# Attention scores of two heads in the two row halves of TensorE's array, with keys that hold no zero blocks

## What is computed

```python
# x: (2, 1024, 256); ctx: (2, 154, 192); 16 heads of 64 features
h = layernorm(x)
q = (h @ Wq).reshape(B, N, 16, 64).transpose(0, 2, 1, 3)
k = (ctx @ Wk).reshape(B, 154, 16, 64).transpose(0, 2, 1, 3)
v = (ctx @ Wv).reshape(B, 154, 16, 64).transpose(0, 2, 1, 3)
sim = einsum('bhid,bhjd->bhij', q, k) * 64 ** -0.5
attn = softmax(sim, axis=-1)
o = einsum('bhij,bhjd->bhid', attn, v)
x = x + tanh(g_xattn) * (o @ Wo + bo)
x = x + tanh(g_ffn) * moe(layernorm(x))   # top 2 of 8 experts, silu gate
```

## Time and profile before

| | |
|---|---|
| timed runs, median of 3 | 596.3 us (595.17 to 599.48) |
| profiled execution, its span (its own time is not told apart) | 602.2 us |
| PE busy (weight loads: 476.4) | 522.3 us, 87% |
| DVE busy | 340.4 us, 57% |
| ACT busy | 282.2 us, 47% |
| POOL busy | 231.9 us, 39% |

### The profile page before, as it was taken

The page is one execution under the profiler, slowest core; times in us unless marked ns, Lnnn a source line. Parts: engine busy times, 40 slices in busy tenths (PEclk is TensorE's granted clock), DMA queues, the critical chain, the costliest instruction groups (busy, mean ns, idle before and its releaser), DMA issues.

```text
span 602.2 us, 12363 instructions
## 1 busy us (share of the span) xinstructions
PE 522.3 (87%) x3712; PEld 476.4 (79%) x3713; DVE 340.4 (57%) x783; ACT 282.2 (47%) x866; POOL 231.9 (39%) x319
## 2 busy tenths in 40 slices
PE   8999999999999999998998420699988998999991
PEld 6789999998989889898998410588877877888881
DVE  5856666677586585765756764255444544533330
ACT  3446556555465555564553112355543544533330
POOL 5160000337008780077704625043433433443333
PEclk9999999999999999999999755799999999999995
DMA  8500000001000100001010995636446436333322
GB/s 246 181 2 1 0 2 2 20 1 35 3 0 26 44 20 15 0 10 63 2 36 1 224 229 178 206 84 151 109 90 156 117 76 157 53 51 53 55 36 26
DMA packets 32372, 41.54 MB, mean 69 GB/s; under 512 B 3088, under 2 KB 28432, under 8 KB 32336
## 3 DMA queue, kind: packets, MB, share of 16 engines
q1 hardware_dynamic: 25184, 31.75, 17.9%
q0 software_dynamic: 7152, 9.33, 9.9%
HBM read 24.12 MB, written 16.95 MB: 68 GB/s over the span
## 4 chain that ended last, share of the span: by engine, by line
PE 34%; issue 26%; DVE 11%; ACT 8%; DMA 6%; POOL 6%; POOLq 3%; DVEq 2%; SPq 2%; another core or an unknown queue 1%; ACTq 0%
PE bank L603 7%; PE bank L581 6%; ACT probs L773 5%; PE bank L527 4%; POOL tok L1225 4%; PE bank L543 4%; PE bank L1279 3%; PE bank L557 3%; DMA expert_queue<-zrow 3%; DVE nmax L892 2%; POOLq L1233 2%; DMA out_dram<-yq,to_row 2%; PE bank L706 2%; PE bank L501 2%; DVEq L902 1%
## 5 line engine op out<-in xcount | busy, mean ns | idle before, releaser
L773 ACT ACTIVATE probs<-bank,nmax 128x154 f32<-128x154 f32 x256 | 97.6, 388 | 123.6 <-DVE nmax L892 119.3
L581 PE MATMUL bank<-vdiag,pT 128*128 128x128 f32 (+2 forms) x640 | 80.0, 272 | 7.1 <-DVE oT_lo L916 6.9
L581 PEld LDWEIGHTS bank<-vdiag,pT 128*128 128x128 f32 (+1 forms) x640 | 77.5, 191 | 10.5 <-DVE oT_lo L916 10.3
L1234 POOL DMA_INDIRECT out_dram<-yq,to_row x39 | 61.8, 1585 | 33.7 <-issue 24.1
L1279 PE MATMUL bank<-gu_hi,xqT_hi 128*128 x156 | 68.7, 441 | 1.1 <-DVE xqT_lo L1396 1.1
L892 DVE TENSOR_REDUCE nmax<-bank 128x2 f32<-128x308 f32 x128 | 60.1, 471 | 7.7 <-PE bank L543 6.8
L1279 PE MATMUL bank<-gu_hi,xqT_lo 128*128 x156 | 61.9, 397 | 0.0
L1279 PE MATMUL bank<-gu_lo,xqT_hi 128*128 x156 | 61.7, 396 | 0.0
L1408 DVE TENSOR_TENSOR hidT_lo<-bank,hidT_hi 128x512 fp32r<-128x512 f32 x39 | 26.9, 690 | 53.1 <-ACT hidT_hi L1355 53.1
L1403 DVE TENSOR_TENSOR hid<-hid,bank 128x512 f32<-128x512 f32 x39 | 26.8, 688 | 52.6 <-PE bank L1279 52.6
L557 PE MATMUL bank<-ident,probs 128*128 128x128 f32 (+1 forms) x320 | 46.2, 273 | 5.6 <-ACT xfT L786 2.9
(11 more groups left out here) (183 smaller groups left out, 1432.4 us busy)
## 6 DMA issues: line engine op xcount, KB each, us to landing
gu_raw<-in_gate_up_wT_dram SPq DMA_DIRECT2D x8, 1024.0 KB, 5.0
expert_queue<-zrow SPq DMA_DIRECT2D x8, 642.5 KB
xq<-expert_queue SPq DMA_DIRECT2D x39, 128.5 KB, 2.5
dn_raw<-in_down_wT_dram SPq DMA_DIRECT2D x8, 512.0 KB, 6.0
x<-in_x_dram SPq DMA_DIRECT2D x4, 512.0 KB, 13.0
out_dram<-out SPq DMA_DIRECT2D x8, 256.0 KB, 2.2
wq_raw<-in_L_xattn_Wq_dram SPq DMA_DIRECT2D x1, 1024.0 KB, 11.5
wo_raw<-in_L_xattn_Wo_dram SPq DMA_DIRECT2D x1, 1024.0 KB, 10.6
```

Of the source, the lines that this page charges most:

```text
L581: last = nc.tensor.matmul(at[:, col0 + j0 * DH:col0 + j0 * DH + n], pT[u % 2][0:rows, b, :], v, start=(b == 0), stop=(b == NBLK - 1), skip ...
L773: last = nc.scalar.activation(probs[u % 4][:, j * NKB:(j + 1) * NKB], S_BANK[hf][:, m * NKB:(m + 1) * NKB], ACT.Exp, bias=nmax[:, u % 4, j ...
L1234: nc.gpsimd.indirect_dma_start(out[:, :], bass.IndirectOffsetOnAxis(to_row[:, 0:1], 0), yq[p % 2][:, :], None, compute_op=ALU.add).then_in ...
```

## The change

The keys lose their zero blocks: `k_hi` and `k_lo` have 154 columns for a pair and batch, the first head in rows 0 to 63 and the second in rows 64 to 127, as PE makes them. The scores of a head are a matmul of 64 array rows and 154 columns: heads of the first half of a pair (`side` 0) go through rows 0 to 63 into `S_BANK[0]`, those of the second half (`side` 1) through rows 64 to 127 into `S_BANK[1]`, in turn. The position in the array follows from the partitions of the operands. A unit has 12 such matmuls in place of 6, and each has its own weight load. Bank 0 now holds the first heads of both pairs, bank 1 the second heads; the maxima write `nmax` with a stride of two and the exponentials find head `2 * m + side` in place `m` of a bank.

All 12 score matmuls of a unit are issued in one piece, ahead of the transpositions, and both semaphores `s["exp"][0]` and `s["exp"][1]` are waited for ahead of the first. ACT and DVE keep their order. The keys are split by one instruction of 128 partitions on ACT and one on DVE, and the memsets of zero blocks and their semaphore are gone. (In the changed file lines stand up to twelve earlier.)

```diff
-            k_hi = asb("k_hi", [P, H // 2, B, 2 * NKB], F32R)
-            k_lo = asb("k_lo", [P, H // 2, B, 2 * NKB], F32R)
+            k_hi = asb("k_hi", [P, H // 2, B, NKB], F32R)
+            k_lo = asb("k_lo", [P, H // 2, B, NKB], F32R)
...
-                for half, keys in zero_keys:
-                    nc.gpsimd.memset(k_lo[half, :, :, keys].bitcast(F32), 0.0).then_inc(s["k_zero"], 1)
-                    nc.gpsimd.drain()
...
                 def scores(i, u):
 
                     par, w = (u // 8) % 2, u % 8
-                    for hf in range(2):
-                        at_least(pe, s["exp"][hf], UPI * i + u)
-                        if w < UPT and hf == 0:
-                            pe.wait_ge(s["proj_sb"][w + 1], GPI * i + u // 8 + 1)
-                        pair = (u % UPT) * 2 + hf
-                        tok = ((u // UPT) % 2) * P
+                    for side in range(2):
+                        at_least(pe, s["exp"][side], UPI * i + u)
+                    if w < UPT:
+                        pe.wait_ge(s["proj_sb"][w + 1], GPI * i + u // 8 + 1)
+                    tok = ((u // UPT) % 2) * P
+                    for m in range(2):
+                        pair = (u % UPT) * 2 + m
                         n = 0
                         for q, k in ((q_hi, k_hi), (q_hi, k_lo), (q_lo, k_hi)):
-                            last = nc.tensor.matmul(S_BANK[hf][:, 0:2 * NKB], q[par][:, pair, tok:tok + P], k[:, pair, par, :],
-                                                    start=(n == 0), stop=(n == 2))
+                            for side in range(2):
+                                rows = slice(side * DH, (side + 1) * DH)
+                                last = nc.tensor.matmul(S_BANK[side][:, m * NKB:(m + 1) * NKB], q[par][rows, pair, tok:tok + P],
+                                                        k[rows, pair, par, :], start=(n == 0), stop=(n == 2))
+                                if m == 1 and n == 2:
+                                    last.then_inc(s["scores"][side], 1)
                             n += 1
-                        last.then_inc(s["scores"][hf], 1)
-                        yield
+                    yield
...
-                    for a in range(2):
-                        half = slice(a * DH, (a + 1) * DH)
-                        last = nc.scalar.activation(k_hi[half, m, :, a * NKB:(a + 1) * NKB],
-                                                    bank[m % 4][half, 0:B * NKB].rearrange("p (b k) -> p b k", b=B), ACT.Copy, scale=SCALE)
-                    last.then_inc(s["k_hi"], 1)
+                    nc.scalar.activation(k_hi[:, m, :, :].rearrange("p b k -> p (b k)"), bank[m % 4][:, 0:B * NKB],
+                                         ACT.Copy, scale=SCALE).then_inc(s["k_hi"], 1)
...
-                            j = 2 * hf + m
+                            j = 2 * m + hf
```

More of the change, by code:

```diff
@@ L104, in gated_xattn_moe @@
                      "out0 out0_q xf xfT_ps logits lg_read lsh ex chosen pos_ps pos_read row_sb rows_q gated pads_q "
-                     "k_zero zero pads order table rows_made zero_q wo_split "
+                     "zero pads order table rows_made zero_q wo_split "
                      "ptA ptB ptA_sb ptB_sb pv y y_sb "
@@ L268, in two_tiles @@
                 return x1[:, first:first + 2, :] if isinstance(i, int) else x1[:, bass.ds(first, 2), :]
-            zero_keys = ((slice(DH, P), slice(0, NKB)), (slice(0, DH), slice(NKB, 2 * NKB)))
             @block.sync
@@ L722, in _ @@
                     first_job(k)
-                pe.wait_ge(s["k_zero"], 3)
                 for u in range(2):
@@ L851, in then @@
                     return ins
-                for half, keys in zero_keys:
-                    last = nc.vector.memset(k_hi[half, :, :, keys].bitcast(F32), 0.0)
-                last.then_inc(s["k_zero"], 1)
                 def token_stats(i, gl):
@@ L891, in maxima @@
                         dve.wait_ge(s["scores"][hf], UPI * i + u + 1)
-                        nc.vector.tensor_reduce(nmax[:, u % 4, 2 * hf:2 * hf + 2], S_BANK[hf][:, 0:2 * NKB].rearrange("p (m k) -> p m k", m=2),
+                        nc.vector.tensor_reduce(nmax[:, u % 4, :].rearrange("p (m side) -> p side m", side=2)[:, hf, :], S_BANK[hf][:, 0:2 * NKB].rearrange("p (m k) -> p m k", m=2),
                                                 AX_X, ALU.max, negate=True).then_inc(s["smax"][hf], 1)
@@ L1084, in _ @@
                     dve.wait_ge(s["k_hi"], m + 1)
-                    for a in range(2):
-                        half, keys = slice(a * DH, (a + 1) * DH), slice(a * NKB, (a + 1) * NKB)
-                        last = nc.vector.scalar_tensor_tensor(k_lo[half, m, :, keys], bank[m % 4][half, 0:B * NKB].rearrange("p (b k) -> p b k", b=B),
-                                                              SCALE, k_hi[half, m, :, keys].bitcast(F32), ALU.mult, ALU.subtract)
-                    last.then_inc(s["k_lo"], 1)
+                    nc.vector.scalar_tensor_tensor(k_lo[:, m, :, :].rearrange("p b k -> p (b k)"), bank[m % 4][:, 0:B * NKB], SCALE,
+                                                   k_hi[:, m, :, :].rearrange("p b k -> p (b k)").bitcast(F32), ALU.mult, ALU.subtract).then_inc(s["k_lo"], 1)
                 def value(b, m):
```

## The result

| | this | before |
|---|---|---|
| timed runs, median | 610.92 us (608.19 to 616.85, 4 runs) | 597.89 us (595.17 to 601.65, 4 runs) |
| ratio | 1.0212 [1.0165, 1.0258] | |
| profiled execution's span | 614.9 us | 602.2 us |
| mean granted clock of PE | 0.940 | 0.952 |

The changed kernel is 2.1% slower. The forecast was 611.0, from a median before of 596.3.

What follows compares the result with a forecast made beforehand. TensorE was taken as the main bound (busy 522 of 602 us), with exponential waits in short slots. Terms +11, -5, +15 and -0.6 gave +20, taken as +15 for overlap: 611 us from 596.3, range 592 to 648.

Steps and rivals of the forecast that it cites:

- Step 1: Attention slot starts: scores wait for both sides' exponentials, 1.4 us a round, +11 us (+6 to +18).
- Step 2: Score matmuls: twelve 154-column products replace six of 308; -0.22 us in three PE-bound slots a round, -5 us.
- Step 3: Array layout switches twice per unit: 0.34 us in three PE-bound slots, about 0.17 in five others; +15 us (0 to +31).
- the overlap: Attention steps partly hide under waits and slack, so the sum of +20 us was taken as +15.
- Step 4: Preparation: fewer key-split instructions let PE's first transposition start earlier; -0.6 us.
- middle case: Score matmuls: both halves load at once, each pair pays the 0.106 us load floor; 0.64 us a unit.
- Rival A: Score matmuls: halves work side by side at streaming rate, switching is free; 583 to 597 us; chance 0.10.
- B: Score matmuls: twelve weight loads of 0.106 us do not overlap; 638 us, or 625 with free switches; chance 0.22.
- C: Score matmuls: 154 columns stream slower per column; 616 us at twice the rate, 650 or more at four; chance 0.10.
- Rival D: Attention: everything cheap cancels, pairs at 0.106 us, free switches, little left of the merged wait; 592 to 602 us; chance 0.20.

Runs made afterwards that it cites:

- merged: Kernel before with both exponential waits ahead of the first score product and all six products of a unit in one piece; 601.78 us, ratio 1.012.
- Tiles_jobs: Changed kernel with both sides' maxima and exponentials side by side, and query jobs 3 and 4 in slots 5 and 6; 605.94 us, ratio 1.0183.
- jobs_early: Kernel before with scores in one piece, separate waits, maxima and exponentials side by side, jobs 3 and 4 one slot later; 591.8 us, ratio 0.9931.
- early_before: Kernel before with scores in one piece, each side keeping its own wait, and maxima and exponentials side by side; ratio 0.9994.
- again: The changed kernel measured and profiled once more, nothing altered; 608.55 us, ratio 1.0233.
- switch: Changed kernel plus one unused 128-row, 8-column product between the two pairs of heads in each unit, adding two layout changes; ratio 1.0491.
- one_piece: Kernel before with all six score products of a unit ahead of the transpositions, each side still waiting for its own exponentials; 597.26 us, ratio 1.0037.
- jobs: Kernel before with query jobs 3 and 4 in slots 5 and 6 instead of 4 and 5; ratio 1.0004.
- early: Changed kernel with both sides' maxima side by side on DVE and their exponentials side by side on ACT; ratio 1.0157.
- Serial: Changed kernel with all six score products of side 0 issued before the six of side 1, not in turn; ratio 1.032.

## Why the prediction was right, step by step

| step | predicted, us | read from rounds or starts, us |
|---|---|---|
| 1, the merged wait | +11 (+6 to +18) | +8.4 (merged, eight rounds), +6.8 (units 0 to 63); timed +7.1 |
| 2 and 3 together, less the overlap | +5 | changed against merged: +3.1 (0.39 a round), +3.4 (units 0 to 63, falls taken off) |
| 4, preparation | -0.6 | -0.5 to -1.5 |
| clock falls | none | +1.7 each, three to five: +5 to +8.5 |
| total | +15 | timed +12.7 (9.9 to 15.4) |

**Step 1** holds, shown by merged. The idle time appeared where it was foreseen, and the slot behind 97.54 went from 3.00 to 3.60, not to 4. The term was 1.4 us a round and measured 1.05, near its lower end of 0.8. The signal arrives 0.10 us after the exponential, where 0.05 was taken. Against that the first delay of 1.12 came out as 0.59, and the long slot of 6.42 gave back 0.92 where 0.6 was taken; that DVE and ACT caught up earlier than taken would account for both, but was not followed in their rows.

**Step 2** holds in its middle case: the two products of a pair start together or 0.03 us apart, and a pair every 0.11 us. Six pairs cost 6 x 0.111 = 0.67 instead of 0.86: -0.19 a slot, where -0.22 was predicted.

**Step 3** holds where PE is the bound. Predicted were 0.34 us for the two changes of a slot; the starts give 0.15 each, 0.09 on the first pair and 0.06 on the second. The net of steps 2 and 3 in such a slot was predicted as +0.12 (0.34 - 0.22) and measured as +0.12 (5.39 to 5.51), +0.13 and +0.13. The part that failed is "about 0.17 in the other five": the same comparison gives +0.01 for those five together, not +0.85. There the shorter block of products (-0.19) and the change ahead of it (+0.15) about cancel. That over-sized the term by 6.8 us in eight rounds; the 5 us taken off the sum for overlap had covered most of it.

**Step 4** holds in its mechanism: PE's first transposition no longer waits for `xn`.

```profile
9.77 4.83 PE L496 MATMUL bank<-ctx_pad,wk 96*128 96x308 f32 x18
14.44 0.60 PE L511 MATMUL bank<-ident,xn 128*128 128x128 f32 x4
```

That profile has the early rise of the clock. Tiles_jobs, with the new keys and the late rise of the kernel before, has that transposition at 17.84, where before has it at 18.36, jobs_early at 18.33 and early_before at 18.49: 0.5 to 0.65 us earlier, as forecast.

```profile
17.84 0.60 PE L511 MATMUL bank<-ident,xn 128*128 128x128 f32 x4
```

What it is worth in the end is harder to read, since the clock rises early or late in the preparation, and that alone moves the first score by 2 us. Among profiles with the late rise (12.5 to 12.9 us) the first score came at 31.54 with the new keys, and at 31.99 to 32.15 with the old ones. Among those with the early rise and no fall behind it, it came at 27.99 to 29.05 (changed, again, switch) and at 29.88 to 30.36 (one_piece, jobs).

**What was missing** is the clock (last section). That the total agrees so closely is luck: two errors cancel. The wait was 2.6 to 4.2 us smaller than taken, steps 2 and 3 another 1.6 to 1.9, and the clock falls cost 5 us or more that no step had. With all rows of the table the total would be 14 to 20 us, above the timed value. Which falls an unprofiled run has is not recorded, but its mean granted clock is: 0.940, 0.947, 0.950 and 0.951 in the four timed runs of the changed kernel. The first of them is the profiled one, with five falls; the profile with three has 0.951. So three to five falls are what these runs allow; it is no close count, since runs of the kernel before, whose profile has none there, lie between 0.946 and 0.959.

Rival A (0.07 a pair, free changes) is excluded by both distances, B by the pairs that start together, C by 0.11 for a pair of 154 columns, where it had at least 0.14. Rival D had the pairs nearly right (0.106) and was wrong on free changes and on little being left of step 1, of which 1.05 us a round stayed. The prediction took two rules from the Trainium skill, "TensorEngine Tiling (Array Packing)", Key Properties. The trace agrees with the second, that different tiles load weights and multiply in parallel: loads and products of a pair both start within 4 ns at 129.72. The first, that a change of tiling mode drains TensorE, was to put step 3 near its upper end of 0.35 us; it measured 0.15, and whether all of the pipe drains is not shown.

## What to carry to other kernels

Two half-height tiles at once did not halve the cost here: a pair of 154 columns took 0.11 us, hardly more than a product of 8 columns (0.106), against 0.143 for the wide product, and one change of layout each way (0.30) ate more than six pairs saved (0.19). At these prices, by an estimate (0.30 us for both changes, 0.03 saved by a pair), at least ten pairs have to stand between two changes before tiles gain anything. Joining two waits ahead of one block, with the order that came with it, cost more a round (1.05 us) than the tiles did (0.39). Before joining, look whether the engine runs ahead on one of them. Issuing both sides together on all three engines with their waits kept apart gave nothing by itself here (0.9994), and moving the jobs gave nothing by itself (1.0004); both together made a kernel 0.7% faster than the one before. And one round is not the whole loop: what moving the jobs saved in plain rounds was mostly paid back in two of those with routing.

## What the runs showed that was not expected

PE's clock fell to half inside the attention part of the changed kernel, for 3.4 us at a time: at 42.3, 55.9, 165.2, 243.7 and 318.8 us in one profile, at 41.2, 54.9 and 164.1 in the other. From unit 0 to unit 63 the first is 3.5 us longer with two more falls, 1.7 us each. The stretch before a fall and the fall itself:

```profile
38.90:42.30 3.40, 1.72 (x19) 1.51 (x19) 1.56 (x5) 2.51 (x10) 2.00 (x3) 1.00 0.00 0
42.30:45.70 3.40, 3.40 (x22) 3.25 (x19) 1.87 (x4) 1.87 (x8) 0.00 (x0) 0.50 0.03 7
```

Ahead of the fall PE was busy 1.72 of 3.40 us, waiting for exponentials, 1.40 us of it in one piece. The merged kernel at the same place was busy a little more and kept its clock, and so did early:

```profile
40.80:44.20 3.40, 1.96 (x14) 1.75 (x15) 1.63 (x4) 2.52 (x10) 2.12 (x3) 1.00 0.02 5
```

```profile
40.10:43.50 3.40, 2.17 (x24) 1.86 (x23) 1.61 (x5) 2.45 (x10) 2.01 (x3) 1.00 0.00 0
```

The kernel before had 3.36 of 3.40 there. A wait on PE may therefore cost twice: its own time, and a slow stretch behind it. But PE's busy time does not tell the falls from the rest. Serial, which has tiles too, fell at 45.1 after 2.00 of 3.40, more than merged's 1.96. Three of the five falls, at 165.2, 243.7 and 318.8, came after 3.40 of 3.40 by the records. What stood there is the same each time, first the sixteen router products of 8 columns, then a block of score pairs:

```profile
161.69 1.85 PE L619 MATMUL bank<-rw,xfT 128*128 128x8 f32 x16
163.46 0.34 PE L541 MATMUL bank<-k_hi,q_hi 64*128 64x154 f32 x2
```

So it is ahead of 164.1 in the second profile of the changed kernel, of 325.0 in serial's and of 172.6, 254.6 and 333.1 in switch's. But the router products at 238.7 and 312.6 in that second profile had no fall behind them, and in merged, where wide score products follow them, the clock stayed. Jobs, without tiles, fell at 165.5 after 1.92 of 3.40, and jobs_early at 166.1, each just behind a wait of 1.4 to 1.8 us for `oT_lo`, while the kernel before, merged and early kept their clock there. What decides stays open; no run was made for it.
